# ScalarE's order in a batch's second block, and the turned heads in halves

## The reference

```
for i in range(6):
    x = attn_layer(shift_tokens(x), Wqkv[i], ...) + x     # 16 heads of 64, windows of 32 tokens
    x = ffn_layer(shift_tokens(x), ln_g[i], ..., W1[i], b1[i], W2[i], b2[i]) + x
# attn_layer: q, k, v = x @ Wqkv; q, k = l2norm * scale, rotary;
#             softmax of 32 queries against their own and the window before; out @ Wo
# ffn_layer:  xn = layernorm(x) * g + b; a, gate = split(xn @ W1 + b1); (a * gelu(gate)) @ W2 + b2
```

## Time and profile before

| | |
|---|---|
| time, median of 3 runs | 2188.56 us (2187.67 to 2188.9) |
| the profiled execution's own time | 2173.51 us |
| its span, first to last instruction | 2171.7 us |
| mean granted TensorE clock | 0.983 |
| PE busy, share of the span | 92% |
| DVE, ACT, POOL busy | 65%, 64%, 50% |

### The profile page before, as it was taken

One profiled execution on the slowest core, in us unless ns is written; L12 is line 12 of the kernel. 1 busy time (PEld: TensorE's weight loads), 2 busy tenths in 40 slices (PEclk: granted clock), 3 DMA queues, 4 the chain that ended last, 5 costly groups with the idle time before them and its releaser, 6 DMA issues.

```text
span 2171.7 us, 74796 instructions
## 1 busy us (share of the span) xinstructions
PE 2003.2 (92%) x32616; PEld 1186.4 (55%) x32616; DVE 1411.9 (65%) x1975; ACT 1397.0 (64%) x2029; POOL 1085.8 (50%) x709
## 2 busy tenths in 40 slices
PE   8999998788999999999999999999999999999997
PEld 5655655355555555555555555555555555555552
DVE  1454444676677776767677767776777676767662
ACT  5555554466677666766676666666766676667763
POOL 0000000586666666556666656665656665666550
PEclk9999998899999999999999999999999999999998
DMA  3000000122223222232222322222322223222220
GB/s 108 2 1 1 2 20 30 37 64 61 60 70 80 75 71 62 58 94 74 72 57 68 90 55 72 73 60 66 80 76 69 62 60 90 70 70 61 61 61 20
DMA packets 82066, 128.11 MB, mean 59 GB/s; under 512 B 17230, under 2 KB 28108, under 8 KB 81740
## 3 DMA queue, kind: packets, MB, share of 16 engines
q1 hardware_dynamic: 81740, 123.33, 21.7%
HBM read 21.55 MB, written 1.05 MB: 10 GB/s over the span
## 4 chain that ended last, share of the span: by engine, by line
PE 70%; ACT 10%; issue 10%; DVE 9%; DMA 0%; ACTq 0%; DVEq 0%; SPq 0%
PE ps L617 13%; PE ps L613 12%; PE ps L639 8%; PE ps L693 6%; PE ps L678 6%; PE ps L685 5%; PE ps L426 3%; PE ps L622 3%; PE ps L626 2%; ACT work L993 2%; PE ps L658 2%; DVE work L1249 2%; DVE SS L1141 2%; PE ps L519 1%; PE ps L440 1%
## 5 line engine op out<-in xcount | busy, mean ns | idle before, releaser
L1418 POOL TENSOR_TENSOR work<-work,RS 128x1024 f32<-128x1024 f32 x192 | 365.2, 1902 | 406.4 <-ACT RS L967 405.1
L1096 DVE TENSOR_TENSOR work<-ps,work 128x512 f32<-128x512 f32 (+1 forms) x288 | 249.1, 865 | 341.1 <-ACT work L1025 304.6
L617 PEld LDWEIGHTS ps<-ident,work 128*128 128x128 f32 x3072 | 344.5, 142 | 167.9 <-issue 120.2
L617 PE MATMUL ps<-ident,work 128*128 128x128 f32 x3072 | 395.3, 276 | 25.9 <-ACT work L993 21.9
L1429 POOL TENSOR_TENSOR work<-work 128x1024 f32<-128x1024 f32 x96 | 226.9, 2364 | 124.9 <-DVE work L1101 124.8
L1437 POOL TENSOR_TENSOR work<-work 128x1024 f32<-128x1024 f32 x96 | 225.9, 2353 | 100.2 <-DVE work L1101 100.2
L1101 DVE TENSOR_TENSOR work<-ps,work 128x512 f32<-128x512 f32 (+1 forms) x288 | 247.3, 859 | 0.0
L1037 ACT ACTIVATE work<-work 128x1024 f32<-128x1024 f32 x96 | 101.5, 1057 | 206.6 <-DVE work L1181 206.3
L1141 DVE TENSOR_REDUCE SS<-work 128x16 f32<-128x1024 f32 x192 | 232.1, 1209 | 0.0
L685 PEld LDWEIGHTS ps<-work 64*32 64x32 f32 x12288 | 134.4, 105 | 148.1 <-issue 132.6
L613 PE MATMUL ps<-WQ,XS 128*128 128x512 f32 x384 | 188.6, 614 | 8.0 <-issue 4.3
(11 more groups left out here) (184 smaller groups left out, 3208.9 us busy)
## 6 DMA issues: line engine op xcount, KB each, us to landing
work<-work SPq DMA_DIRECT2D x576, 128.0 KB
work<-work SPq DMA_DIRECT2D x336, 64.0 KB
WQ<-in_wqkv SPq DMA_DIRECT2D x6, 512.0 KB, 3.7
WK<-in_wqkv SPq DMA_DIRECT2D x6, 512.0 KB, 4.5
WV<-in_wqkv SPq DMA_DIRECT2D x6, 512.0 KB, 3.5
WO<-in_wo SPq DMA_DIRECT2D x6, 512.0 KB, 3.9
work<-ZR SPq DMA_DIRECT2D x48, 64.0 KB
W<-in_w SPq DMA_DIRECT2D x6, 341.0 KB, 3.1
```

The costliest lines, as they stand in the source:

```text
L617: m = nc.tensor.transpose(flat(R)[:, t * 128:t * 128 + 128], src[:, t * 128:t * 128 + 128], ident[:, :])
L1096: V.tensor_tensor(h16(cos_part[:, j, cols]), h16(src), rotary_tabs[:, at:at + 64].unsqueeze(1).broadcast_to([PARTS, heads_in, 64]), ALU.mu ...
L1418: U.tensor_tensor(h16(qk_norm[:, j, :]), h16(cos_part[:, j, :]), inv_norms[:, j, :].unsqueeze(2).broadcast_to([PARTS, 16, 64]), ALU.mult). ...
```

## The change

In the second block of a batch the keys' inverse norms of the block before leave the end of the first step and stand behind the copy of the heads, ahead of the GELU tables. The first GELU stands directly behind the table load, and the copy of the values behind it. In all blocks the turning of the heads signals after each half of its eight transposes, the copy into `heads_t` is done as two activations of four transposes each, and the first and second half of the keys' turning wait for the first and second half of that copy. The counts of the semaphores follow.

```diff
--- before.py
+++ after.py
@@ -632,7 +632,7 @@
             def project_out(f, first, last):
                 if first == 0:
                     pe.wait_ge(wo_loaded, 16 * (f // 4 + 1))
-                    pe.wait_ge(heads_turned_copied, 4 * f + 4)
+                    pe.wait_ge(heads_turned_copied, 8 * f + 8)
                     if due(f):
                         pe.wait_ge(gate_gelu, 3 * f)
                 for k in range(first, last):
@@ -698,7 +698,8 @@
                     hid(0, bank_f)
                 if d:
                     pe.wait_ge(heads_copied, g - 2)
-                    turn(bank_y, heads).then_inc(heads_turned, 1)
+                    turn(bank_y, heads, 0, 4).then_inc(heads_turned, 1)
+                    turn(bank_y, heads, 4, 8).then_inc(heads_turned, 1)
                 if f is not None and n == 0:
                     centre(f)
                 if f is not None and n == 1:
@@ -710,10 +711,10 @@
                     project_out(fo, 3, 6)
                 if b:
                     pe.wait_ge(k_normed, g)
-                    if d:
-                        pe.wait_ge(heads_turned_copied, g - 2)
-                    turn(bank_y, qk_norm[:, 1, :], 0, 4).then_inc(k_turned, 1)
-                    turn(bank_y, qk_norm[:, 1, :], 4, 8).then_inc(k_turned, 1)
+                    for half in range(2):
+                        if d:
+                            pe.wait_ge(heads_turned_copied, 2 * g - 5 + half)
+                        turn(bank_y, qk_norm[:, 1, :], 4 * half, 4 * half + 4).then_inc(k_turned, 1)
                 if f is not None and n == 1:
                     pe.wait_ge(gate_gelu, 3 * f + 2)
                     hid_gate(2, bank_f)
@@ -953,7 +954,7 @@
             def copy_heads(g):
                 act.wait_ge(heads_weighed, g - 1)
                 if due(g - 2):
-                    act.wait_ge(heads_turned, g - 2)
+                    act.wait_ge(heads_turned, 2 * g - 4)
                 A(heads.rearrange('p (c q d) -> p q c d', q=2, d=64), bank_y.rearrange('p q (c d) -> p q c d', d=64), ACT.Copy).then_inc(heads_copied, 1)
 
 
@@ -976,21 +977,23 @@
                 if d:
                     copy_heads(g - 1)
                 if f is not None and n == 1:
+                    if b:
+                        invert_norms(g - 1, 1)
                     nc.scalar.preload_act_table_set(GELU)
+                    gelu(f, 0, bank_f)
                 if b:
                     act.wait_ge(values_ready, g)
                     if due(g - 1):
                         act.wait_ge(windows_loaded, 160 * (g - 1))
                     A(v_rows[:, (n - 1) % 2, :], flat(bank_x), ACT.Copy).then_inc(values_copied, 1)
-                if f is not None and n == 1:
-                    gelu(f, 0, bank_f)
                 if d:
-                    act.wait_ge(heads_turned, g - 2)
                     bt = (g - 3) // 4
                     slot = 4 if bt % 2 and n == 3 else (g - 3) % 4
                     if due(bt - (n == 3)):
                         act.wait_ge(attn_projected_out, bt - (n == 3))
-                    A(heads_t[:, :, slot * 128:slot * 128 + 128], turned(bank_y), ACT.Copy).then_inc(heads_turned_copied, 1)
+                    for half in range(2):
+                        act.wait_ge(heads_turned, 2 * g - 5 + half)
+                        A(heads_t[:, 4 * half:4 * half + 4, slot * 128:slot * 128 + 128], bank_y[:, half, :].rearrange('p (c t) -> p c t', t=128), ACT.Copy).then_inc(heads_turned_copied, 1)
                 if f is not None and n == 1:
                     gelu(f, 1, bank_f)
                 if b:
@@ -1035,7 +1038,8 @@
                     if due(g - 1):
                         act.wait_ge(probs_turned, g - 1)
                     A(probs[:, :, :, :], scores_sb[:, :, :, :], ACT.Exp).then_inc(probs_exp, 1)
-                if a:
+
+                if a and not (f is not None and n == 0):
                     invert_norms(g, 1)
 
             def last_square(b):
```

## The result

The kernel after the change takes 2094.6 us (median of 4 runs, 2089.9 to 2098.3) against 2188.1 us of the kernel before (2182.9 to 2188.9): a ratio of 0.9579, 95% interval 0.9556 to 0.9602, 93 us less (87 to 97 by the interval). The profiled execution took 2094.7 us, its span is 2092.9 us, and its mean clock 0.990. Between the two profiled executions the difference is 78.8 us.

What follows compares the result with a forecast made beforehand. TensorE, busy 92% of the span, was taken as the bound, with gains only from its waits and lower clock. 51.7 (order) + 12 (clock) + 15 (halves) = 79 us off 2188.6 gave 2110 us, range 2093 to 2143.

Steps and rivals of the forecast that it cites:

- the halves: Keys' turning no longer waits for the whole heads' copy: 0.34 us from each of 44 places, 15 us.
- the clock: TensorE's seven falls to 1.2 GHz behind the waits for `gated` go, 1.7 us each: 12 us.
- The order of ScalarE: Second block: earlier first GELU removes TensorE's wait for `gated` in 22 places, 2.45 us each less 0.1: 51.7 us.
- The rival with 1.4 us more on the GELU: Second block, GELU behind the table load: part of the wait for `gated` stays, 2143 us; 14 in 100.
- The keys on GpSimd: Second block: keys' product 0.1 us later, margin 2.7 us; if too late, slower, 22 us per microsecond; 4 in 100.
- the 15 us going too: Median's 15 us above the profiled execution are further clock falls behind the other 15 waits: 2095 us; 7 in 100.

Runs made afterwards that it cites:

- the order alone: Kernel before with ScalarE's new order in the second block, heads turned, signalled and copied in one piece: 2102.6 us, ratio 0.9635.
- the halves alone: Kernel after with ScalarE's order as before, heads still turned and copied in two halves: 2170.6 us, ratio 0.9948 against the kernel before.
- the built-in wait: Kernel after with four unread 128x512 SBUF copies on ScalarE ahead of the GELU tables' load in 22 blocks: 2167.2 us.
- the last series: Kernel after unaltered, 2091.2 us, beside the same with the two last-layer-norm additions moved behind step g = 97 on VectorE, 2091.0 us.
- the last additions behind: Kernel after with the two last-layer-norm additions (L1206) behind step g = 97 on VectorE instead of ahead: 2088.7 us, then 2091.0 us.

## Why the prediction was right, and where its sizes were off

The forecast was 2110 us with a range of 2093 to 2143; 2094.6 lies at its lower edge. The way was right, and two terms of the sum were off, in opposite directions: the halves were worth less than forecast and the clock more.

*The order of ScalarE: right, term by term.* 51.7 us were forecast from 22 x (2.45 - 0.1). The row of waits lost all of the 54.0 us, since VectorE is ready 0.03 us before TensorE rather than 0.1 us after. The timeline followed the forecast within 0.16 us at every step. The two experiments that undo one half of it each show that both halves are needed: 1.55 us stay without the norms, 0.8 us without the GELU. That there is no margin shows in them too, as a delay of the GELU by 0.9 us is a wait of 0.8 to 0.95.

*The drain behind a table load: not seen.* The rival with 1.4 us more on the GELU didn't come. The Trainium skill, "ScalarE: Activation LUTs", "What ACT_TABLE_LOAD costs", adds some 1380 ns of drain to the load; here the load ended at 811.28 and the GELU began at 811.30, and ahead of the load 0.01 us passed from the end of the norms (809.99) to its start. The measurement decides.

*The keys on GpSimd: right.* The margin of 2.7 us was read correctly: 2.6 us of delay are free, 6.7 us are not. The price that I gave, 22 us for each microsecond beyond, was too low, as it left out the clock: 128 us for 3.8 us in each of 22 blocks is 34 us for each.

*The halves: right in kind, the term too large.* 15 us were forecast; alone they give 11 us (7 to 15), and on top of the order 8 to 11. The step that failed is "their first half is needed some 1.75 us after the start of the turning, which is about when it comes". It does come then: 831.62 to 833.39, 1.77 us. But it is needed sooner. 1.75 us is about where the first matmul of the keys' projection starts (923.38 in the trace before, 1.78); its weight load starts at 1.67, and 0.11 us more go by between the end of the copy and the load, so the copy would have to end at 1.56. It comes 0.21 us too late, and the load, which had no idle time ahead of it, has 0.19. So of the 0.39 us that the turning starts earlier, 0.21 are kept, as the stretch from the heads' turning to the scores shows: 5.87 us before and with the order alone, 5.66 in the kernel after, by the median of all first and of all third blocks. In 44 places that is 9 us. That the sum took 0.34 of the 0.39 us had no row behind it at this point.

*The clock: right in kind, the term too small.* 12 us were forecast, from the seven falls of the one profiled execution, and the 15 us between that execution and the median were carried over unexplained. A good part of them was of the same kind. The kernel before has 29 executions that came with a mean clock, the profiled one and those beside the experiments. The profiled one was the fastest, 2173.5 us at 0.983; the three slowest took 2189.9 to 2190.0 us at 0.973; in between the five at 0.977 took 2184.7 us on average, the seven at 0.979 2180.7 us. The median is 2182.5 us, 9 us above the profiled one, which at 1.7 us each is 5 to 6 falls more: 12 or 13 behind the 22 waits. I count 13 in the profiled executions of the halves alone and of the built-in wait, which have these waits at about this length. With 13 it is 22 us and not 12. No execution of the kernel before at its median speed left a trace, so where its further falls lie is inferred, not seen. I had named this case, the 15 us going too, with a chance of 7 in 100 and 2095 us. It should have had far more: a fall was possible at each of the 22 waits, and one profile showed one draw of them.

*The sum as measured.* 54 (waits) + 9 (halves) + 22 (clock) = 85 us against 93 measured in the first series, and 2183.2 - 2091.2 = 92 in the last. The mean clocks say much the same of the clock's share: with 1 minus the clock, times the span, as the work lost, the 29 executions before lost 48.6 us on average and the eight of the kernel after 24.6, which is 24 us. That leaves 5 to 8 us in none of the terms. The interval of the last series, 0.9556 to 0.9601, is 5 us wide to either side, so little of that is clear of noise, and no run here tells where it is.

Between the two profiled executions 54 + 9 + 12 = 75 of 78.8 us are accounted for, and the clock accounts for the rest, away from the 22 waits. Behind the last of them the kernel before spent 14.0 us at 1.2 GHz and the kernel after 7.0; ahead of the six layers it was 37.5 and 34.1 us. Half of the difference is work lost: 3.5 and 1.7 us. The sum is then 80 us, 1 us too much. That part looks like chance and not like a gain of the change: a second profiled execution of the kernel after, in the last series, has 10.5 us in place of 7.0 and 37.5 in place of 34.1, and ahead of the layers, which the change doesn't touch, the other kernels have between 34.1 and 41.0 us.

## What to carry to other kernels

When the chain that ends last leads out of the busiest engine and back, list what each queue on that way does ahead of the instruction that is waited for, and ask of each piece who needs it when: here a small piece that waited for another engine, and a large copy whose own reader came later, both stood ahead of a GELU that TensorE needed first. Where a wait is taken away, what stands behind it is needed sooner by as much: work out from which instruction that need counts (here a weight load, not the matmul behind it) and what the release costs, and take "about when it comes" for a term that has yet to be worked out. Where a profiled execution is faster than the median, compare their clocks before carrying the difference over: a wait that sometimes brings a fall of the clock costs more in the runs than in that one profile.

## What the runs showed of the hardware

How often TensorE's clock fell to 1.2 GHz behind or in an idle stretch grew with its length, over 22 waits in each profiled execution: none with 0.8 us on average (0.94 at most), 4 with 1.55 us on average (all four at 1.69 or 1.70 us), 7 in one execution and 13 in each of two others with 2.1 to 2.6 us, and all 22 with 3.7 to 3.85 us, ten of these twice as long. Short stretches are not safe in every case: the kernel after has ten idle stretches of 0.77 to 1.24 us between 500 and 2030 us and no fall in that time, with TensorE busy for 1514.9 of 1530 us, but one of 1.21 us, in the run with the last additions behind, had a fall 0.3 us after it. One fall of the shorter kind is 3.4 us at 1.2 GHz, 1.7 us of work where TensorE is busy throughout.

A product of 128x512 on GpSimd, tied only to the one before it, took 1.27 us on average over 110 of them, and five in a row 6.67 us; I had reckoned 1.04 to 1.06 us each from a row of the stage ahead of the layers.
